# Reordering the head of a fused attention and FP4 feed-forward kernel: late pieces of x as jobs, zero rows by GpSimd, zeros multiplied in waits

## The chip, the cores and the metric

The kernel runs on one core of a Trainium2 chip. The metric is the device time of one execution in microseconds, the median of the runs shown. A core has a matrix engine (TensorE, PE in the profile), a vector engine (VectorE, DVE), a scalar engine that applies functions such as SiLU (ScalarE, ACT), a general engine (GpSimd, POOL) and a queue that mostly starts transfers (SyncE, SP). Each works through its own list of instructions in order, and they wait for one another by semaphores.

## The reference, cut to what matters

The input x has 2048 rows of 128 features.

```python
x_proj = silu(x @ W1 + b1)                      # (2048, 512)
u, v, q, k = split(x_proj, 4)                   # 16 heads of 8 features
scores = einsum('bqhd,bkhd->bhqk', qh, kh)      # 16 x 2048 x 2048
attn = silu(scores) / S
av = einsum('bhqk,bkhd->bqhd', attn, vh)
x = layernorm(x + (layernorm(av * u, gamma, beta) @ W2 + b2))
h = silu(fp4(x) @ fp4(w_gate).T) * (fp4(x) @ fp4(w_up).T)
out = layernorm(x + fp4(h) @ fp4(w_down).T)
```

SiLU is applied to every one of the 16 x 2048 x 2048 scores, 67 million values.

## The kernel before

**Layout.** x comes in five pieces (`X_LOADS`), is turned by TensorE against an identity matrix (L433) and copied from PSUM to `xT`. `k` and `q` are projected from `xT` in fp32, pass SiLU on ScalarE (`feat`) and are split by VectorE into three bf16 parts (`split`, L724 to L729). Transfers then lay these parts down in `k_stack` and `q_stack`, eight rows per head feature (`stack`, L255): six rows are products of parts, the last two must be zero. Such zero rows come from a memset for the first 256 columns (L864, L865, semaphore `stack_zeroed`) and from a transfer out of `zeros` for the others (`zero_rows`, L246). A unit is one such piece of k or q: (k, 0), (q, 0), (k, 256), (k, 768), (k, 1280), (k, 1792), and then the q pieces. The first three units are stacked half by SP and half by GpSimd (`SHARES`), the others by SP alone.

**The head.** `HEAD` (L226) is a list of operations (kind, start, width, PSUM bank) that TensorE goes through in order; after each one ScalarE takes the bank over (L649 to L660), a copy for `xT` and a SiLU for k, q and v. All five pieces of x, both first pieces of v and three pieces of k are in this list. Ahead of it stand six products of zeros (`WARM_UP`).

**The loop.** 256 steps (`STEPS`) go over chunks of queries, groups of heads and 16 tiles of keys. A step is `scores(at)`, two halves of 8 small products each into banks 0 to 5, taken by ScalarE with one SiLU of 128x1024 for a half (L682), then `times_v(at - 2)`, which multiplies the result of two steps ago by `v_pad`. Half n may be written only when SiLU n - 3 is done. Step i of the first chunk needs key tile i, so step 2 waits for the stack of (k, 256), step 6 for (k, 768), step 10 for (k, 1280) and step 14 for (k, 1792); `times_v(4)`, at step 6, needs the second v.

**Jobs.** `PREP_AT` says behind which step TensorE does a remaining piece of work: step: (kind, start). Before a job TensorE waits until the job before it has been taken out of its bank (`wait_job(k - 1)`, L518). ScalarE takes k, q, v and u jobs over after the first SiLU of the next step (L683, L684); VectorE takes the others.

**GpSimd and VectorE in the head.** GpSimd builds the identity, zeroes `v_pad` for the first four tiles (L314), prepares v's bias (L322 to L327), starts its share of the stack transfers, and copies v into `v_pad` (`pad_v`). VectorE zeroes small buffers, splits k and q, and zeroes the later quarters of `v_pad` between (`zero_v`).

## Time and profile before

| | |
|---|---|
| median of 3 runs | 520.77 us (518.68 to 522.34) |
| profiled execution | 521.81 us, of which the span from first to last instruction is 519.9 us |
| mean granted TensorE clock | 0.994 |
| PE busy | 500.2 us (96%) |
| ACT busy | 490.8 us (94%) |
| DVE busy | 210.8 us (41%) |
| POOL busy | 55.2 us (11%) |

Times in the rows are microseconds from the start of the span. Busy means that an instruction was running; an engine can be 96% busy and still be ahead of the one that sets the pace. A timeline row merges like instructions that follow each other: its second number is from the start of the first to the end of the last.

### The profile page before, as it was taken

To read this page: it belongs to the slowest core of one execution; us is meant where nothing else is said; L and a number is where in the kernel's file an instruction comes from. 1 tells how busy PE (TensorE), PEld (TensorE's weight loads), DVE (VectorE), ACT (ScalarE), POOL (GpSimd) and SP (SyncE) were. 2 spreads that over 40 slices of the span, in tenths; PEclk is the share of its full clock that TensorE was granted. 3 is DMA by queue.
4 is the path that set the end of the run, shared out by engine and by line. 5 is a ranking of instruction groups with operands and counts; after the bars stand their busy time and mean duration, and the time that the engine had idled before them with its cause. 6 is when DMAs were issued, how large, how long until landed. Compare 5 with 4: busy or idle time off the path is not lost.

```text
span 519.9 us, 19994 instructions
## 1 busy us (share of the span) xinstructions
PE 500.2 (96%) x9011; PEld 263.6 (51%) x9012; DVE 210.8 (41%) x621; ACT 490.8 (94%) x557; POOL 55.2 (11%) x148
## 2 busy tenths in 40 slices
PE   8899999999999999999999999999999999999995
PEld 4443344444444444444444444444367777777762
DVE  5446652343343332334333333334343434444445
ACT  4899999999999999999999999999999999999940
POOL 6600000101010100101010100101010101101010
PEclk9899999999999999999999999999999999999999
DMA  7831440000000000000000000000000000000000
GB/s 179 211 89 49 112 118 27 3 3 6 3 7 3 7 3 6 3 1 8 1 8 3 6 3 6 3 2 8 1 9 4 9 5 9 9 3 9 4 3 11
DMA packets 15155, 12.38 MB, mean 24 GB/s; under 512 B 1783, under 2 KB 14718, under 8 KB 15070
## 3 DMA queue, kind: packets, MB, share of 16 engines
q1 hardware_dynamic: 14088, 9.44, 7.2%
q0 software_dynamic: 688, 1.40, 1.1%
q8 instruction: 71, 1.16, 0.9%
q10 hardware_dynamic: 294, 0.26, 0.2%
q14 instruction: 14, 0.11, 0.1%
HBM read 1.92 MB, written 1.05 MB: 6 GB/s over the span
## 4 chain that ended last, share of the span: by engine, by line
ACT 54%; PE 31%; issue 11%; DVE 2%; DMA 1%; POOL 0%; SPq 0%; POOLq 0%; DVEq 0%
ACT attn L625 54%; PE ps L390 29%; PE ps L404 2%; DMA x_sb<-in_L_attn_x 1%; PE ps L433 0%; ACT v_sb L625 0%; POOL rstd_b L373 0%; DVE xn_b L751 0%; DVE stats_b L781 0%; ACT feat L625 0%; DVE xn_b L755 0%; DVE xn_b L757 0%; DVE xn_b L759 0%; SPq L275 0%; POOLq L126 0%
## 5 line engine op out<-in xcount | busy, mean ns | idle before, releaser
L625 ACT ACTIVATE attn<-ps 128x1024 f32<-128x1024 f32 x512 | 479.1, 1220 | 1.7 <-PE ps L390 1.5
L390 PE MATMUL ps<-attn,v_pad 128*32 128x256 f32 (+1 forms) x5120 | 275.2, 342 | 0.3 <-DVE wdown_t L925 0.2
L390 PE MATMUL ps<-q_stack,k_stack 64*128 64x256 bf16 (+1 forms) x2560 | 175.8, 251 | 11.8 <-ACT attn L625 2.6
L390 PEld LDWEIGHTS ps<-attn,v_pad 128*32 128x32 f32 x5120 | 132.4, 109 | 80.7 <-issue 39.4
L390 PEld LDWEIGHTS ps<-q_stack,k_stack 64*128 64x128 bf16 x2560 | 77.6, 94 | 138.1 <-ACT attn L625 93.5
L372 POOL TENSOR_TENSOR ve_a<-mv_a,eps_col 128x1 f32<-128x1 f32 x24 | 4.6, 190 | 244.5 <-DVE mv_a L783 244.5
L840 DVE TENSOR_TENSOR gate_a<-gate_a,ps 128x352 f32<-128x352 f32 x8 | 4.2, 521 | 53.1 <-PE ps L390 53.1
L372 POOL TENSOR_TENSOR ve_b<-mv_b,eps_col 128x1 f32<-128x1 f32 x24 | 4.6, 190 | 192.5 <-DVE mv_b L783 192.5
L840 DVE TENSOR_TENSOR gate_b<-gate_b,ps 128x352 f32<-128x352 f32 x7 | 3.7, 522 | 48.0 <-PE ps L390 48.0
L724 DVE CAST parts<-feat 128x512 bf16<-128x512 f32 (+1 forms) x10 | 3.9, 388 | 26.7 <-ACT feat L625 26.7
L390 PE MATMUL ps<-zeros 128*128 128x512 bf16 x47 | 12.2, 411 | 1.3 <-DVE zeros L862 1.2
L373 POOL TENSOR_TENSOR rstd_a<-ve_a,minus_half 128x1 f32<-128x1 f32 x24 | 13.3, 554 | 1.9
L373 POOL TENSOR_TENSOR rstd_b<-ve_b,minus_half 128x1 f32<-128x1 f32 x24 | 13.3, 553 | 1.9
L848 DVE COPY hqT_a<-ps 128x256 f32<-128x256 f32 x8 | 3.4, 424 | 22.4 <-PE ps L404 22.4
L390 PE MATMUL ps<-wgate_t,xqT 128*32 128x352 f32 (+1 forms) x122 | 12.5, 460 | 0.0
L390 PE MATMUL ps<-wup_t,xqT 128*32 128x352 f32 (+1 forms) x122 | 12.4, 459 | 0.0
L834 DVE COPY xqT<-ps 128x128 f32<-128x128 f32 x15 | 4.4, 292 | 16.9 <-PE ps L390 16.9
L848 DVE COPY hqT_b<-ps 128x256 f32<-128x256 f32 x7 | 3.0, 425 | 19.4 <-PE ps L404 19.4
L390 PE MATMUL ps<-xT,w_qk 128*32 128x512 f32 (+3 forms) x56 | 10.8, 582 | 0.0
L781 DVE BATCH_NORM_STATS2 stats_a<-ps 128x6 f32<-128x128 f32 x8 | 2.4, 299 | 19.4 <-PE ps L390 19.4
L625 ACT ACTIVATE feat<-ps,b_col 128x512 f32<-128x512 f32 (+1 forms) x10 | 7.5, 753 | 2.7 <-PE ps L390 2.7
L854 DVE TENSOR_TENSOR x1p_a<-ps,x_a 128x128 f32<-128x128 f32 x7 | 2.0, 292 | 19.6 <-PE ps L390 19.6
(156 smaller groups left out, 344.7 us busy)
## 6 DMA issues: line engine op xcount, KB each, us to landing
q_stack<-parts SPq DMA_DIRECT2D x18, 128.0 KB, 2.4
k_stack<-parts SPq DMA_DIRECT2D x15, 128.0 KB, 3.6
x_sb<-in_L_attn_x SPq DMA_DIRECT2D x3, 256.0 KB, 6.5
k_stack<-zeros SPq DMA_DIRECT2D x6, 128.0 KB, 5.5
q_stack<-zeros SPq DMA_DIRECT2D x6, 128.0 KB, 2.4
k_stack<-parts SPq DMA_DIRECT2D x9, 64.0 KB, 3.0
q_stack<-parts SPq DMA_DIRECT2D x9, 64.0 KB, 2.0
out<-x_a SPq DMA_DIRECT2D x8, 64.0 KB, 1.5
```

The source lines that it names most:

```text
L372: link(pool.tensor_tensor(r.ve[:, :], r.mv[:, which, 1:2], eps_col[:, :], ALU.add))
L373: pool.tensor_tensor(r.rstd[:, which:which + 1], r.ve[:, :], minus_half[:, :], ALU.pow).then_inc(rstd_ready, 1)
L390: return pe.matmul(to, lhsT, rhs, start=start, stop=stop, skip_group_check=True)
L404: return pe.transpose(ps[0:m, bank, a:a + n], src[:, 0:m], ident[0:n, 0:n])
L625: return act.activation(to, frm, ACT.Silu, **kw)
L724: dve.tensor_copy(p[:, 0, :], f).then_inc(split_done, 1)
L781: dve.bn_stats(r.stats[:, :], src)
L834: dve.tensor_copy(xqT[:, tile % 2, :], ps[:, bank, 0:P]).then_inc(job_by_vec, 1)
L840: dve.tensor_tensor(r.gate[:, :], r.gate[:, :], ps[:, bank, 0:FF], ALU.mult).then_inc(job_by_vec, 1)
L848: dve.tensor_copy(r.hqT[:, 0:2, :].rearrange("p t n -> p (t n)"), ps[:, bank, 0:2 * P])
L854: dve.tensor_tensor(r.x1p[:, :], ps[:, bank, 0:D], r.x1[:, :], ALU.add).then_inc(job_by_vec, 1)
```

## The change

1. `HEAD` loses the pieces (xT, 1280), (xT, 1792) and (v, 512); (k, 256) stands ahead of (xT, 768). The three become jobs at steps 1, 4 and 0. The other jobs up to (up, 0) stand one step later than before.
2. The last two pieces of x are loaded by SP behind the stacks of units 0 and 1 instead of ahead of them. They are turned by `turn_x` and copied by VectorE (`copy_xT`) instead of ScalarE.
3. The zero rows of unit 2, (k, 256), come from a GpSimd memset of columns 256 to 768 of `k_stack` (all eight rows, 8 x 512 bf16 for each partition) instead of two transfers by SP. GpSimd and SP wait for `k_zeroed`.
4. The first quarter of `v_pad` is zeroed half by GpSimd, two tiles, and half by VectorE, two tiles, behind the copy of `b1_col` (L873).
5. `FILL`: TensorE multiplies zeros once behind (xT, 0), three times behind (xT, 256), both into bank 7, and five times behind (k, 768) into bank 4.

The diff without the lines that only rename:

```diff
--- before.py
+++ after.py
@@ -92,9 +92,9 @@
 
-    PREP_AT = {2: ("k", 1280), 5: ("v", 2), 7: ("k", 1792), 9: ("v", 3), 11: ("u", 0), 13: ("q", 256),
-               15: ("u", 1), 17: ("q", 512), 19: ("u", 2), 21: ("q", 1024), 23: ("u", 3), 25: ("q", 1536),
-               27: ("w2", 0), 29: ("gate", 0), 31: ("up", 0), 33: ("down", 0)}
+    PREP_AT = {0: ("v", 1), 1: ("xT", 1280), 3: ("k", 1280), 4: ("xT", 1792), 6: ("v", 2), 8: ("k", 1792), 10: ("v", 3),
+               12: ("u", 0), 14: ("q", 256), 16: ("u", 1), 18: ("q", 512), 20: ("u", 2), 22: ("q", 1024),
+               24: ("u", 3), 26: ("q", 1536), 28: ("w2", 0), 30: ("gate", 0), 32: ("up", 0), 33: ("down", 0)}
 
     WIDE, DENSE = KT - 6, KT - 2
@@ -204,8 +204,8 @@
         split_done = sem("split_done")
-        stack_zeroed, v_zeroed_early, v_zeroed, v_padded = (sem("stack_zeroed"), sem("v_zeroed_early"), sem("v_zeroed"),
-                                                            sem("v_padded"))
+        stack_zeroed, k_zeroed, v_zeroed_early = sem("stack_zeroed"), sem("k_zeroed"), sem("v_zeroed_early")
+        v_zeroed, v_padded = sem("v_zeroed"), sem("v_padded")
         stacked = [sem(f"stacked{n}") for n in range(len(UNITS))]
         scores_ready, attn_ready = sem("scores_ready"), sem("attn_ready")
@@ -223,13 +223,14 @@
 
-        HEAD = [("xT", 0, 256, 0), ("k", 0, 256, 1), ("q", 0, 256, 2), ("xT", 256, 512, 3), ("xT", 768, 512, 4),
-                ("k", 256, 512, 5), ("xT", 1280, 512, 7), ("xT", 1792, 256, 0), ("v", 0, 512, 6),
-                ("k", 768, 512, 7), ("v", 512, 512, 6)]
+        HEAD = [("xT", 0, 256, 0), ("k", 0, 256, 1), ("q", 0, 256, 2), ("xT", 256, 512, 3), ("k", 256, 512, 5),
+                ("xT", 768, 512, 4), ("v", 0, 512, 6), ("k", 768, 512, 7)]
+
+        FILL = {("xT", 0): (1, 7), ("xT", 256): (3, 7), ("k", 768): (5, 4)}
         B1U_BANK = 2
         head_no = {job[:2]: n for n, job in enumerate(HEAD)}
-        X_LOADS = [(job[1], job[2]) for job in HEAD if job[0] == "xT"]
+        X_LOADS = [(0, 256), (256, 512), (768, 512), (1280, 512), (1792, 256)]
         xT_all = max(n for n, job in enumerate(HEAD) if job[0] == "xT") + 1
 
@@ -256,11 +257,10 @@
         SHARES = [((0, 1, 4), (2, 5, 3)), ((0, 2, 5), (1, 4, 3)), ((0, 1, 4), (2, 5, 3))]
-        BY_DMA = [len(SHARES[0][0]), len(SHARES[1][0]), len(SHARES[2][0]) + HD - TERMS]
 
             if n < len(SHARES):
-                eng.wait_ge(stacked[n], 16 * BY_DMA[n])
+                eng.wait_ge(stacked[n], 16 * len(SHARES[n][0]))
                 eng.wait_ge(stacked_by_pool[n], 16 * len(SHARES[n][1]))
                 eng.wait_ge(stacked[n], 16 * HD)
@@ -280,13 +280,14 @@
             load_x(sp, 2)
+            sp.wait_ge(stack_zeroed, 2)
+            for n in range(2):
+                stack(sp, n, SHARES[n][0])
+            load_x(sp, 3)
+            load_x(sp, 4)
+            sp.wait_ge(k_zeroed, 1)
+            stack(sp, 2, SHARES[2][0])
             sp.wait_ge(zeros_ready, 1)
-            for n in range(3, len(X_LOADS)):
-                load_x(sp, n)
-            zero_rows(sp, unit_no[("k", 256)])
-            sp.wait_ge(stack_zeroed, 2)
-            for n in range(3):
-                stack(sp, n, SHARES[n][0])
             for start in (768, 1280, 1792):
                 stack(sp, unit_no[("k", start)])
@@ -311,7 +312,8 @@
                                base=0, pattern=[[-1, P]], channel_multiplier=1).then_inc(ident_ready, 1)
-            pool.memset(v_pad[:, 0:TPC, :, :], 0.0).then_inc(v_zeroed_early, 1)
+            pool.memset(k_stack[:, :, 256:768], 0.0).then_inc(k_zeroed, 1)
+            pool.memset(v_pad[:, 0:2, :, :], 0.0).then_inc(v_zeroed_early, 1)
             pool.memset(ones_row[:, :], 1.0)
             pool.memset(minus_half[:, :], -0.5)
@@ -327,6 +329,7 @@
             pool.wait_ge(stack_zeroed, 2)
+            pool.wait_ge(k_zeroed, 1)
             for n in range(3):
 
@@ -335,7 +338,7 @@
                 else:
-                    pool.wait_ge(v_zeroed_early, 1)
+                    pool.wait_ge(v_zeroed_early, 2)
                 if ("v", c * CH) in head_no:
                 else:
@@ -418,9 +421,18 @@
 
+            def turn_x(bank, start, w):
+                pe.wait_ge(x_loaded[X_LOADS.index((start, w))], 16)
+                for i in range(w // P):
+                    last = pe.transpose(ps[:, bank, i * P:(i + 1) * P], x_sb[:, start // P + i, :], ident[:, :])
+                return last
+
+            def multiply_zeros(times, bank):
+                for _ in range(times):
+                    mm(ps[:, bank, :], zeros[:, 0:P], zeros[:, :])
+
             pe.wait_ge(zeros_ready, 1)
-            for _ in range(WARM_UP):
-                mm(ps[:, 7, :], zeros[:, 0:P], zeros[:, :])
+            multiply_zeros(WARM_UP, 7)
             pe.wait_ge(ident_ready, 1)
             for n, (kind, start, w, bank) in enumerate(HEAD):
@@ -428,9 +440,7 @@
                 if kind == "xT":
-                    pe.wait_ge(x_loaded[X_LOADS.index((start, w))], 16)
-                    for i in range(w // P):
-                        last = pe.transpose(ps[:, bank, i * P:(i + 1) * P], x_sb[:, start // P + i, :], ident[:, :])
+                    last = turn_x(bank, start, w)
                 else:
                                              if job[0] == "xT" and job[1] < start + w) + 1)
@@ -449,6 +459,7 @@
                     mm(ps[:, B1U_BANK, 0:1], b1_rows, ident[0:4, 0:1]).then_inc(b1_made, 1)
+                multiply_zeros(*FILL.get((kind, start), (0, 0)))
             pe.wait_ge(head_act, xT_all)
 
@@ -523,6 +534,8 @@
                     last = behind(kind, tile, bank)
+                elif kind == "xT":
+                    last = turn_x(bank, i, X_LOADS[[a for a, _ in X_LOADS].index(i)][1])
                 elif kind == "u":
                 elif kind in ("q", "k"):
@@ -589,8 +602,7 @@
             def keep_warm(piece):
-                for _ in range(KEEP_WARM.get(piece, 0)):
-                    mm(ps[:, 2, :], zeros[:, 0:P], zeros[:, :])
+                multiply_zeros(KEEP_WARM.get(piece, 0), 2)
 
             wait_job(job_no[("hqT", 0, TAIL - 1)])
@@ -871,6 +883,12 @@
             dve.tensor_copy(b1_col[:, 1:3], ps[:, 6, 1:3]).then_inc(b1_ready, 1)
+            dve.memset(v_pad[:, 2:TPC, :, :], 0.0).then_inc(v_zeroed_early, 1)
+
+            def copy_xT(start):
+                bank = wait_made("xT", start, None)
+                w = X_LOADS[[a for a, _ in X_LOADS].index(start)][1]
+                dve.tensor_copy(xT[:, start:start + w], ps[:, bank, 0:w]).then_inc(job_by_vec, 1)
 
                 dve.memset(v_pad[:, c * TPC:(c + 1) * TPC, :, :], 0.0).then_inc(v_zeroed, 1)
@@ -881,8 +899,10 @@
             split("k", 768)
+            copy_xT(1280)
             zero_v(1)
             split("k", 1280)
+            copy_xT(1792)
             zero_v(2)
```

## Rows read from the trace of the kernel before

**Rows 1.** The page, busy time, share and instructions of each engine

```profile
PE 500.2 (96%) x9011; PEld 263.6 (51%) x9012; DVE 210.8 (41%) x621; ACT 490.8 (94%) x557; POOL 55.2 (11%) x148
```

**Rows 2.** The page's costliest group: busy us, mean ns, then idle before it

```profile
L625 ACT ACTIVATE attn<-ps 128x1024 f32<-128x1024 f32 x512 | 479.1, 1220 | 1.7 <-PE ps L390 1.5
```

**Rows 3.** Waits of ACT from 30 to 500 us: total, times, longest

```profile
ACT attn L625 <- PE ps L390: 0.2, 1, 0.2
```

**Rows 4.** ACT's timeline: start, duration, instruction, idle before and its releaser

```profile
16.69 5.60 ACT L625 ACTIVATE attn<-ps 128x1024 f32<-128x1024 f32 x6
23.63 1.02 ACT L625 ACTIVATE attn<-ps 128x1024 f32<-128x1024 f32 x1 [1.34 <-PE ps L390]
24.55 0.68 ACT L625 ACTIVATE feat<-ps,b_col 128x512 f32<-128x512 f32 x1
...
29.97 1.02 ACT L625 ACTIVATE attn<-ps 128x1024 f32<-128x1024 f32 x1 [0.16 <-PE ps L390]
30.89 0.59 ACT L625 ACTIVATE v_sb<-ps 128x512 f32<-128x512 f32 x1
31.36 3.78 ACT L625 ACTIVATE attn<-ps 128x1024 f32<-128x1024 f32 x4
```

**Rows 5.** PE's timeline in the head, and one v job in the loop

```profile
1.19 2.74 PE L390 MATMUL ps<-zeros 128*128 128x512 bf16 x6 [1.19 <-DVE zeros L862]
...
5.00 2.07 PE L390 MATMUL ps<-xT,w_qk 128*128 128x256 f32 x4
6.87 1.06 PE L433 MATMUL ps<-ident,x_sb 128*128 128x128 f32 x4
8.63 1.12 PE L433 MATMUL ps<-ident,x_sb 128*128 128x128 f32 x4 [0.70 <-DMA x_sb<-in_L_attn_x]
9.54 1.92 PE L390 MATMUL ps<-xT,w_qk 128*128 128x512 f32 x2
...
11.90 1.09 PE L433 MATMUL ps<-ident,x_sb 128*128 128x128 f32 x6
12.82 1.06 PE L390 MATMUL ps<-w_sb,xT 128*128 128x128 f32 x8
...
13.94 1.02 PE L390 MATMUL ps<-xT,w_qk 128*128 128x512 f32 x2
...
16.09 0.83 PE L390 MATMUL ps<-q_stack,k_stack 64*128 64x256 bf16 x12
...
28.33 1.06 PE L390 MATMUL ps<-w_sb,xT 128*32 128x128 f32 x32
```

**Rows 6.** Two stretches, PE alone: length, busy (instructions), granted clock, DMA share, GB/s

```profile
16.09:20.13 4.04, 2.15 (x25) 0.89 0.99 240
20.13:23.20 3.07, 3.07 (x27) 0.59 1.08 234
```

**Rows 7.** PE's timeline in the tail, a run of products of zeros

```profile
502.20 4.70 PE L390 MATMUL ps<-zeros 128*128 128x512 bf16 x21 [0.16 <-issue]
```

**Rows 8.** SP's timeline, stack transfers of units 1 and 2

```profile
9.09 1.90 SPq L255 DMA_DIRECT2D q_stack<-parts  x3
12.66 2.45 SPq L255 DMA_DIRECT2D k_stack<-parts  x3
```

**Rows 9.** POOL's timeline, the memset that is cut and its first stack transfers

```profile
1.43 1.80 POOL L314 MEMSET v_pad<- 128x2048 f32 x1
...
7.70 1.77 POOL L255 DMA_DIRECT2D k_stack<-parts  x3 [0.88 <-DVE parts L724]
```

**Rows 10.** DVE's timeline, a memset of 1024 words and the first split

```profile
2.51 0.91 DVE L865 MEMSET q_stack<- 128x1024 uint32 x1 [0.16 <-issue]
...
6.76 0.29 DVE L724 CAST parts<-feat 128x256 bf16<-128x256 f32 x1 [1.53 <-ACT feat L625]
```

**Rows 11.** Q_stack's transfers issued from 10 to 12 us: time to landing

```profile
DMA to landing us min/median/max: 2.9/3.5/4.0
```

**Rows 12.** X_sb's transfers issued from 3.2 to 3.8 us: time to landing

```profile
DMA to landing us min/median/max: 7.3/7.3/7.4
```

## The prediction, made before the result was known

> **What bounds the kernel now.** I read the busy times first [rows 1]: PE 96% and ACT 94%, so either could set the pace. The group that costs most tells which: 512 SiLUs of scores take 479.1 us of ACT, and ACT stood idle ahead of them for 1.7 us in all [rows 2]. From 30 to 500 us its only wait for PE is 0.2 us [rows 3], and that is the one of 0.16 us at 29.97 [rows 4]. So from the first score SiLU, at 16.69, ACT is the clock of the whole kernel, one SiLU per 0.90 us or so (five more starts in a run of 5.60 us with a last one of about 1.02: 4.6 / 5 = 0.92). PE's 96% is slack spread thin. The reader should see three places where time can be had: the start at 16.69, the stalls of 1.34 and 0.16 us behind it (1.50 together) [rows 4], and other work on ACT between score SiLUs. The tail isn't touched. All else in the head counts only by what it does to these.
>
> What sets 16.69? PE's list of operations in the head [rows 5]. PE is busy almost without a break to the first scores at 16.09, and the first SiLU starts 0.60 us after them. The one visible gap is 0.70 us ahead of 8.63, where it waits for the third piece of x. Beside the order there is the clock: the same kind of product of 128x512 fp32 takes 1.92 us at 9.54 and 1.02 us at 13.94, and the four turns at 8.63 take 1.12 us where six take 1.09 us at 11.90. So PE ran at its lower level, 1.2 GHz, until about 11.5, and at 2.4 GHz behind it, though the granted clock of the first microseconds is shown as full. The trace has a second such stretch: over 16.09 to 20.13 PE was busy for only 2.15 of 4.04 us, and in 20.13 to 23.20 the granted clock is 0.59 [rows 6]. There lies the stall of 1.34 us: PE had times_v(0), the k job of step 2 and then the scores that ACT waited for, all at or near the lower level.
>
> **The change, part by part: the start.** I add up PE's list anew.
> - One product of zeros behind the first turn. A zero costs 2.74 / 6 = 0.46 us at the lower level [rows 5]; most lies in the wait for ACT's copy of xT, which k needs. Bounds 0 to 0.46, I take 0.2. The four turns of (xT, 256) then end at 7.93 + 0.20 = 8.13.
> - Three zeros, of which the wait for the copy (about 0.6 us) hides less than half at this level: 3 x 0.46 = 1.37, to 9.50. At the upper level a zero costs 4.70 / 21 = 0.22 us [rows 7] and the three fit the wait.
> - (k, 256) now runs here. Between 1.02 and 1.92 us; I take 1.02, since PE has by then been busy from 5.0 without the gap of 0.70, and before it rose some 2.9 us after that gap. To 10.52. The small b1 product behind it: 11.90 - 11.46 = 0.44, to 10.96.
> - (xT, 768), its load there since 8.6: 4 / 6 of 1.09 = 0.73, to 11.69. (v, 0): from 12.82 to 13.94, 1.12, to 12.81. (k, 768): 1.02, to 13.83; ACT's copy of (xT, 768), due by 12.4, doesn't hold it up. Gone are (xT, 1280), (xT, 1792) and (v, 512).
> - Five zeros at 0.22: 1.12, to 14.95. First SiLU 0.60 later: 15.55. That is 1.15 us earlier.
> The cover of this is the landing of the first two stacks. SP's transfers of q go out until 10.99 [rows 8], and those issued from 10 us landed 2.9 to 4.0 us later [rows 11], so at about 14.4: hidden behind 14.95, but a faster list than this gains at most 0.5 us more. With two loads of x and two zero transfers no longer ahead of them these landings should not get longer.
>
> **GpSimd and VectorE.** GpSimd's memset of 2048 words took 1.80 us [rows 9]. Now it does 8 x 512 bf16, as 2048 words another 1.80 us, or as 4096 elements 3.6 us, and then half of v_pad, 0.9 us. That puts its queue back by 0.9 us or by 2.7 us. Behind it stand v's bias, then the shares of the stacks of units 0, 1 and 2. Its first transfer was held back 0.88 us by the first split [rows 9], so a delay of 0.9 us costs nothing, one of 2.7 us puts the q share back by 1.8 us. The nearest row for the form is VectorE's zero memset of 8 x 256 bf16, shown as 1024 uint32 [rows 10]; I take the packed form.
>
> The Trainium skill (VectorE: DVE Perf Modes, section "Zero memsets can be issued as uint32 (trn2)") says that a memset takes one cycle an element whatever the type and describes the uint32 form for the Vector engine. Read strictly, GpSimd's would run over 4096 elements; that is one of the rivals below.
>
> VectorE's half of v_pad is 1024 words, 0.91 us by its row, in an idle time of 1.53 us ahead of the first split [rows 10]: nothing. If that cover were gone it would put back every stack by as much.
>
> **SP.** The two late loads of x stand between the stacks of unit 1 and unit 2, about 1.0 us of issuing from 10.99; unit 2's share then goes from 12.0 to some 13.8 instead of 12.66 to 15.11 [rows 8], and lands near 17, where step 2 wants it at about 19. The third and fourth piece of x were under way for up to 7.3 us [rows 12]; issued at 11.0 they land by 18.3 at the very worst, by 15 more likely. Both are hidden by what comes next.
>
> **The loop.** (v, 1) is now between score SiLUs: its row at 30.89 is followed by the next at 31.36, so 0.47 us of ACT, in full on the path. The copies of xT went to VectorE, which has time. The new thing is that two jobs stand in neighbouring steps. Job 1 (turn x 1280) waits for ScalarE to have taken job 0, and ScalarE does that only behind the first SiLU of step 1. Queued behind this wait on PE are the scores of step 2. By the sum: SiLU 2 from 17.35, v from 18.25 to 18.85, turns 0.73, scores 0.4 and on to ACT 0.2, so SiLU 4 at about 20.2, where ACT is free at 19.65: 0.55 us lost. The same pair stands at steps 3 and 4, with only two turns (0.36 us) and a k that ACT holds for 0.68 us [rows 4]: 0.2 us, and 0.15 for the k job itself. New stalls 0.9 us, bounds 0.3 to 1.8. In return PE has more to do right behind the head, v's 1.06 + 0.14 us (its row at 28.33) and the turns, so that the empty stretch that preceded the fall of the clock is half as long; I take the old 1.50 us as gone. Later jobs come one step later: (k, 1792) lands about 1.8 us later for step 14, which I count as still hidden, and the others have more room.
>
> Sum: -1.15 (start) - 1.50 (old stalls) + 0.90 (new ones) + 0.47 (v) = -1.28 us. The profiled execution took 521.81 us with a span of 519.9; this makes 520.5 with a span of 518.6. The median shown is 1.0 us lower than that execution, so 520.77 - 1.28 = 519.5.
>
> **The rivals.**
> - The clock rises early, and the fills cost nothing: zeros at 0.22, start held by the stacks at about 15.0 (-1.7), and only 0.4 us of new stalls. -1.7 - 1.5 + 0.4 + 0.47 = -2.3: 518.4. For it: PE's list has no gap left. Against it: it was busy from 1.19 to 7.93 already and stayed low.
> - Slower than before: the clock stays low. If (k, 256) takes 1.92 us, the first SiLU comes at 16.45 (-0.25), and if the fall of 20.13 to 23.20 comes again, the old 1.50 us stay and the new 0.90 are added. -0.25 + 0.90 + 0.47 = +1.1: 521.9. It decides as soon as the score stretch brings the lower level back. For it: zeros at the lower level are themselves work ahead of k. Against: the fall followed a stretch that is now fuller. The Trainium skill (TensorE: Matmul & The Clock Gate, section "What's actually happening") calls the throttled state the default that activity releases, which the turn from 1.92 to 1.02 us bears out; by it both this case and the one above are open.
> - GpSimd's memset by elements: q's share is last issued near 12.3 instead of 10.5 and lands at 15.3 to 16.3, so the first scores start at about 15.8, 0.85 later than in my sum: 519.5 + 0.85 = 520.4, the change without effect.
>
> **How the numbers follow.** The forecast has 0.4, the early rise 0.2, the low clock 0.2, the slow memset 0.2. The forecast is the likeliest's, 519.5. The range takes in the two outer cases, widened by the bounds of the new stalls on either side: 517.6 to 522.0. A measurement of this kernel can tell about 1% from no change, 5.2 us. All the time that this change could free, start and stalls together, is some 3.5 us, and no case costs over 2; outside 1% either way only an effect that I haven't seen would bring it: 0.03 each.
>
> **What would show each step.** First score SiLU at 15 to 16 instead of 16.69; the product for (k, 256) at about 9.5 with 1.0 us; a SiLU of v between the third and the fourth score SiLU; an idle time of ACT of about half a microsecond ahead of the fifth; the granted clock at 1.00 over the stretch that ends the first five steps; the GpSimd memset at 1.8 us. Wrong would make it a wait of the first scores for a stack, a wait of step 14 for (k, 1792), or a fall of the clock.

## The result and the profile after

The changed kernel's median is 522.89 us over 20 runs (521.78 to 526.43); that of before, over 20 runs beside it, is 520.55 us (518.68 to 522.66). The ratio is 1.0054 with a 95% interval of 1.004 to 1.0067: about 2.8 us slower by the ratio, 2.3 by the medians. Forecast was 519.5 us, 1.3 us faster, with a range of 517.6 to 522.0.

The profiled execution of the changed kernel took 521.78 us with a span of 519.8 us, and that of before 519.9. Compared alone these two would say that nothing happened. First ACT's timeline of the changed kernel (columns as in [rows 4], whose counterpart this is):

```profile
16.68 2.86 ACT L637 ACTIVATE attn<-ps 128x1024 f32<-128x1024 f32 x3 [0.72 <-PE ps L393]
19.40 0.62 ACT L637 ACTIVATE v_sb<-ps 128x512 f32<-128x512 f32 x1
...
21.09 3.77 ACT L637 ACTIVATE attn<-ps 128x1024 f32<-128x1024 f32 x4 [0.16 <-PE ps L393]
25.04 1.02 ACT L637 ACTIVATE attn<-ps 128x1024 f32<-128x1024 f32 x1 [0.17 <-PE ps L393]
...
31.68 1.02 ACT L637 ACTIVATE attn<-ps 128x1024 f32<-128x1024 f32 x1 [0.41 <-PE ps L393]
...
33.08 3.78 ACT L637 ACTIVATE attn<-ps 128x1024 f32<-128x1024 f32 x4
```

The start of the first score SiLU hasn't moved (16.68 against 16.69). The stall of 1.34 us is gone, small ones of 0.16, 0.17 and 0.41 stand in the loop now, and v (19.40) is between the third and the fourth score SiLU. PE's timeline, the counterpart of [rows 5]:

```profile
5.95 0.58 PE L393 MATMUL ps<-ident,magic_b 4*128 4x2 f32 x2 [1.37 <-DVE magic_b L880]
...
6.87 1.91 PE L393 MATMUL ps<-xT,w_qk 128*128 128x256 f32 x4
...
9.43 1.49 PE L393 MATMUL ps<-zeros 128*128 128x512 bf16 x3
10.71 1.65 PE L393 MATMUL ps<-xT,w_qk 128*128 128x512 f32 x2
...
15.07 1.24 PE L393 MATMUL ps<-zeros 128*128 128x512 bf16 x5
16.24 0.61 PE L393 MATMUL ps<-q_stack,k_stack 64*128 64x256 bf16 x8
...
20.07 0.66 PE L427 MATMUL ps<-ident,x_sb 128*128 128x128 f32 x4 [1.45 <-ACT v_sb L637]
```

k's first product starts at 6.87 instead of 5.00, and PE waits 1.37 us for a small copy by VectorE. In before the two small copies there were these:

```profile
3.78 0.27 DVE L868 COPY magic_b<-gate_b 4x128 f32<-4x128 f32 x1 [0.22 <-DMA gate_b<-in_L_attn_b]
3.98 0.26 DVE L871 COPY w_qk<-w_sb 128x128 f32<-128x128 f32 x1
```

VectorE and GpSimd of the changed kernel show what became of them (for the memsets see [rows 9 and 10]). VectorE:

```profile
1.43 0.91 DVE L876 MEMSET k_stack<- 128x1024 uint32 x1 [0.16 <-issue]
2.50 0.91 DVE L877 MEMSET q_stack<- 128x1024 uint32 x1 [0.16 <-issue]
...
3.77 2.12 DVE L880 COPY magic_b<-gate_b 4x128 f32<-4x128 f32 x1 [0.21 <-DMA gate_b<-in_L_attn_b]
3.96 2.00 DVE L883 COPY w_qk<-w_sb 128x128 f32<-128x128 f32 x1
```

GpSimd, of the same execution:

```profile
1.43 3.50 POOL L315 MEMSET k_stack<- 128x4096 bf16 x1
4.88 0.94 POOL L316 MEMSET v_pad<- 128x1024 f32 x1
...
9.57 1.77 POOL L256 DMA_DIRECT2D k_stack<-parts  x3 [0.82 <-DVE parts L736]
11.33 1.56 POOL L256 DMA_DIRECT2D q_stack<-parts  x3
```

The memset went over 4096 elements and took 3.50 us. The two copies of 0.27 and 0.26 us stand on VectorE as 2.12 and 2.00 us long, and both end within 0.15 us of the end of GpSimd's second memset (4.88 + 0.94 = 5.82). I call this the hold below; that GpSimd's memsets are its cause is tested by e12. VectorE's own memsets at 1.43 and 2.50 ran beside GpSimd's at their usual 0.91. And GpSimd's own stack transfers start at 9.57 instead of 7.70.

**Where in the span the time is.** One subtraction settles much. The row of four score SiLUs behind the third v (`x4`, at 33.08 above) is followed by 519.8 - 33.08 = 486.7 us to the end. In the experiments with the changed order of jobs below it is 518.9 - 32.23, 517.0 - 30.28, 515.8 - 29.11 and 522.6 - 35.91: 486.7 each time. In the order of before it is 519.9 - 31.36 = 488.5 [rows 4], and for another execution of before 517.2 - 28.64 = 488.6 (two SiLUs more, since v comes one step earlier). So all differences between the profiled executions, of different kernels and of one kernel, arise in the first 36 us.

### The profile page after: what moved, and what is told of

Read it like the earlier page. It is cut to its first block, busy times and chain, and to the rows that moved or that the text cites. A ratio compares the mean times of both kernels' runs of the same rounds, so it can differ in the third digit from the quotient of the medians.

```text
span 519.8 us, 20067 instructions
## 1 busy us (share of the span) xinstructions
PE 499.7 (96%) x9048; PEld 264.1 (51%) x9048; DVE 214.5 (41%) x624; ACT 490.1 (94%) x555; POOL 58.8 (11%) x149
## 3 DMA queue, kind: packets, MB, share of 16 engines
HBM read 1.92 MB, written 1.05 MB: 6 GB/s over the span
## 4 chain that ended last, share of the span: by engine, by line
ACT 52%; PE 32%; issue 10%; DVE 2%; DMA 1%; SPq 1%; POOL 0%; POOLq 0%; DVEq 0%
ACT attn L637 52%; PE ps L393 30%; PE ps L407 2%; SPq L256 1%; DMA k_stack<-parts 1%; PE ps L427 0%; DMA gate_b<-in_L_attn_b 0%; DVE magic_b L880 0%; ACT feat L637 0%; POOL rstd_b L376 0%; DVE xn_b L763 0%; DVE stats_b L793 0%; DVE xn_b L767 0%; DVE xn_b L771 0%; DVE xn_b L769 0%
## 5 line engine op out<-in xcount | busy, mean ns | idle before, releaser
L393 PE MATMUL ps<-zeros 128*128 128x512 bf16 x57 | 15.8, 423 | 1.2 <-DVE zeros L874 1.2
L393 PEld LDWEIGHTS ps<-zeros 128*128 128x128 bf16 x57 | 5.9, 106 | 8.2 <-issue 2.4
```

The lines of the kernel that those rows point to most:

```text
L393: return pe.matmul(to, lhsT, rhs, start=start, stop=stop, skip_group_check=True)
```

## The experiments

Each kernel was timed together with before. The medians of before in the four groups were 520.09 (e1 to e4), 520.18 (e5 to e8), 520.39 (e9 to e12) and 518.81 us (e13 to e15, 15 runs); 20 to 30 runs each in the first three. The last column counts the executions whose mean granted clock was under 0.996, which a fall to the lower level for some 3 us gives: of the profiles kept, those of before, e4, e12 and e14 have such a mean and show such a fall in the head, and no other shows one in its first 34 us.

The four groups ran on four chips, so a difference of medians across groups is less exact than one within a group. Before's own executions with a clock of 0.996 or more had medians of 519.2, 518.8, 518.7 and 518.5 us in the four groups, up to 0.7 us apart. I give the ratios to before beside such differences where they matter.

| kernel | median, us | ratio to before (95%) | first score SiLU, us | clock under 0.996 |
|---|---|---|---|---|
| changed | 522.89 | 1.0054 (1.004 to 1.0067) | 16.68 | 8 of 20 |
| e1_packed | 522.4 | 1.0045 (1.0027 to 1.0063) | 13.68 | 7 of 12 |
| e2_pool_only | 521.38 | 1.0011 (0.9994 to 1.0029) | 17.86 | 5 of 12 |
| e3_no_fill | 524.28 | 1.0089 (1.0066 to 1.0113) | 16.41 | 5 of 6 |
| e4_v_in_head | 522.86 | 1.006 (1.0037 to 1.0082) | 17.18 | 3 of 6 |
| e5_packed_x_early | 519.04 | 0.9989 (0.9975 to 1.0004) | 13.88 | 0 of 12 |
| e6_jobs_apart | 518.08 | 0.9974 (0.9962 to 0.9987) | 13.53 | 0 of 12 |
| e7_before_filled | 519.71 | 1.0002 (0.9989 to 1.0015) | 15.59 | 0 of 12 |
| e9_x_early_only | 520.88 | 1.002 (1.0002 to 1.0038) | 16.01 | 0 of 12 |
| e10_apart_no_fill | 519.53 | 0.9986 (0.9968 to 1.0003) | 15.06 | 0 of 12 |
| e11_apart_v_in_head | 519.51 | 0.9984 (0.9964 to 1.0004) | 16.45 | 5 of 12 |
| e12_copies_by_max | 524.42 | 1.0068 (1.0042 to 1.0095) | 16.48 | 7 of 7 |
| e13_gap_filled | 522.3 | 1.0057 (1.0037 to 1.0077) | 16.95 | 1 of 10 |

The start of the first score SiLU is that of the one profiled execution.

**e1_packed** (from the changed kernel):

```diff
-            pool.memset(k_stack[:, :, 256:768], 0.0).then_inc(k_zeroed, 1)
+            pool.memset(k_stack[:, :, 256:768].bitcast(U32), 0).then_inc(k_zeroed, 1)
```

> The changed kernel with GpSimd's memset of k_stack's columns 256 to 768 over the same bytes as 2048 uint32 instead of 4096 bf16. Theory (the memset holds VectorE's first two copies, which end at 5.9 instead of 4.2, and with them k and the whole head): the memset takes 1.8 us instead of 3.50, the copies end at about 4.2, k's first product starts at 5.3 instead of 6.87, the first score SiLU comes 1.4 to 1.6 us earlier than 16.68, and the median falls by as much, to about 521.4. Rival (the lost time is in the loop, by the added SiLU of v and the jobs in neighbouring steps): the start moves but ACT's stalls behind it grow by the same, and the median stays within 0.4 us of 522.9.

The mechanism was right and the forecast of the time wrong; the time came out nearer to the rival's. The memset took 1.80 us, VectorE's copies 0.34 and 0.25 us, k's product started at 4.85, and the first score SiLU came 3.0 us earlier, twice what was expected, since the clock was up earlier too (k's first product 1.13 us instead of 1.91).

```profile
1.43 1.80 POOL L315 MEMSET k_stack<- 128x2048 uint32 x1
...
4.04 0.25 DVE L883 COPY w_qk<-w_sb 128x128 f32<-128x128 f32 x1
```

Yet the span fell by 0.9 us and the median by 0.5, which the intervals of the two ratios do not tell apart. ACT's and PE's timelines show what took its place:

```profile
13.68 2.85 ACT L637 ACTIVATE attn<-ps 128x1024 f32<-128x1024 f32 x3 [1.72 <-PE ps L393]
...
19.57 3.77 ACT L637 ACTIVATE attn<-ps 128x1024 f32<-128x1024 f32 x4 [1.63 <-PE ps L393]
```

```profile
13.25 0.61 PE L393 MATMUL ps<-q_stack,k_stack 64*128 64x256 bf16 x8 [0.93 <-DMA q_stack<-parts]
...
19.14 0.61 PE L393 MATMUL ps<-q_stack,k_stack 64*128 64x256 bf16 x8 [1.40 <-DMA k_stack<-parts]
```

Step 2 waits for the stack of (k, 256). Its last five transfers, issued from 11.5 to 13.1 us, took this long to land:

```profile
DMA to landing us min/median/max: 5.0/5.8/6.0
```

SP had issued the late loads of x, its last two pieces, just ahead of them. And from 6 to 8 us, when in before these loads were under way, the transfers stood nearly still (columns: stretch, length, PE busy (count), clock, DMA share, GB/s):

```profile
6.00:7.00 1.00, 1.00 (x7) 1.00 0.02 6
7.00:8.00 1.00, 0.96 (x3) 1.00 0.03 6
```

**e2_pool_only**, from before: `pool.memset(k_stack[:, :, 256:768], 0.0)` ahead of the whole v_pad memset, the two zero transfers of unit 2 gone, with the waits that go with it.

> The kernel before with one part of the change: GpSimd's memset of 4096 bf16 in place of unit 2's two zero transfers, ahead of the whole v_pad memset. Theory (a GpSimd memset holds VectorE's copies): GpSimd zeroes without a break from 1.43 to about 6.7, VectorE's two copies that ended at 4.2 end at about 6.7, k's first product starts at 7.7 instead of 5.00, the first score SiLU comes 2.3 to 2.7 us later than 16.69 and the median rises by about as much, to 523. Rival (only GpSimd's own queue is late, its stack transfers by 3.5 us): VectorE's copies stay at 0.27 us, and scores wait for q's stack, at most 1 us later.

```profile
4.02 2.73 DVE L871 COPY magic_b<-gate_b 4x128 f32<-4x128 f32 x1 [0.46 <-DMA gate_b<-in_L_attn_b]
4.21 2.61 DVE L874 COPY w_qk<-w_sb 128x128 f32<-128x128 f32 x1
```

VectorE's copies ended within 0.15 us of the end of GpSimd's memsets (6.68); k's product started at 7.32. The hold is thus there in the old order too. The first score SiLU came 1.2 us later than in the rows of before, but 2.5 us later than in another execution of before (e8, below), which is the size expected. The median rose by 1.3 us, half of what I had expected, and the interval of the ratio takes in 1. The twelve executions fall into two sets, and the five with a clock under 0.996 are the faster ones here, 520.2 to 520.3 us against 521.3 to 522.0. So a low mean clock is no loss by itself. The profile is one of the others, and no trace shows what the five do differently.

**e3_no_fill**, from the changed kernel: `FILL = {}`.

> The changed kernel without the nine products of zeros in the head. Theory (the clock rises at the same place anyway, and the five zeros behind (k, 768) stand in front of the first scores): the first score SiLU comes about 1.2 us earlier, and the median falls by 0.8 to 1.2 us. Rival (the zeros hold the clock up through the first scores): the product of (k, 256) goes back to 1.9 us, a granted clock of 0.5 appears for about 3 us between 17 and 24 in most executions, and the median rises by 1 us or more.

The rival held, as far as it was seen. (k, 256) took 2.08 us, and though the first score SiLU came 0.27 us earlier, the median rose by 1.4 us. Five of six executions had a clock under 0.996. The profiled one had not, so the fall itself is here read from the executions' clocks, not from rows.

**e4_v_in_head**, from the changed kernel: `("v", 512, 512, 6)` at the end of `HEAD`, no job at step 0.

> The changed kernel with the second v back at the end of the head's list, behind the zeros, and no job at step 0. Theory (its place behind the start is worth what it costs): PE's list is 1.2 us longer, the first score SiLU comes 1.2 us later, ACT saves 0.47 us for v and some 0.5 us of the wait of job 1 for job 0: the median is within 0.5 us of the changed kernel's. Rival (the pair of jobs at steps 0 and 1 is the loss): the median falls by 1 us or more.

As in the theory: 522.86 against 522.89.

**e5_packed_x_early**, from e1_packed:

```diff
             load_x(sp, 2)
+            load_x(sp, 3)
+            load_x(sp, 4)
             sp.wait_ge(stack_zeroed, 2)
             for n in range(2):
                 stack(sp, n, SHARES[n][0])
-            load_x(sp, 3)
-            load_x(sp, 4)
```

> e1_packed with one more part undone: the last two loads of x again go out ahead of the stacks. Theory (in e1 the transfers stood nearly still from 6 to 8 us, and then the late loads went out just ahead of unit 2's stack, which took 5.9 us to land and held ACT's fifth SiLU back by 1.63 us): the landing of unit 2's stack falls to 3 to 4 us, ACT's wait ahead of the fifth score SiLU to 0.2 to 0.6 us, and the median is about 1 us below e1's 522.4. Rival (the loads cost the first stacks what they spare unit 2's): the first score SiLU goes from 13.7 to 14.5 or later, and the median stays.

It gave more than the theory said, 3.4 us by the medians (e1 and e5 ran in different groups), 2.9 by the ratios. The same five transfers of unit 2's stack landed within 3.3 to 4.6 us, against 5.0 to 6.0 in e1. SP also issued its three of them 1.2 us earlier, from 10.7 instead of 11.9, and no run parts the two. The wait of 1.63 us is one of 0.16; the first SiLU stays at 13.88; and no execution has a low clock any more. Its executions lie within 518.63 to 519.38 us, those of e1 within 520.0 to 524.45. The five of e1 with a clock of 0.996 or more have a median of 520.8, so some 1.7 us are there without a fall of the clock.

```profile
DMA to landing us min/median/max: 3.3/3.7/4.6
```

```profile
13.88 2.85 ACT L637 ACTIVATE attn<-ps 128x1024 f32<-128x1024 f32 x3 [1.79 <-PE ps L393]
...
18.30 3.77 ACT L637 ACTIVATE attn<-ps 128x1024 f32<-128x1024 f32 x4 [0.16 <-PE ps L393]
```

**e6_jobs_apart**, from e5:

```diff
-    PREP_AT = {0: ("v", 1), 1: ("xT", 1280), 3: ("k", 1280), 4: ("xT", 1792), 6: ...
+    PREP_AT = {0: ("v", 1), 2: ("xT", 1280), 3: ("k", 1280), 5: ("xT", 1792), 6: ...
```

> e5_packed_x_early with the jobs (xT, 1280) at step 2 and (xT, 1792) at step 5 instead of 1 and 4, so that none directly follows a job of ScalarE. Theory (PE stands for 1.4 us for job 0's SiLU and 0.5 us for that of the k job, which holds ACT back and lets the clock fall in a part of the executions): both gaps go, the sum of ACT's waits from the first score SiLU to 35 us falls by 0.5 to 0.9 us, fewer executions have a granted clock under 0.996, and the median falls by 1 to 1.5 us. Rival (the waits are those for stacks, the gap only shows them): no change over 0.3 us.

The waits behind the first SiLU are down to one of 0.16 us, the median falls by 1.0 us. The part about the clock could not be tested, for e5 had no low execution left. This is the version that beats both kernels: 518.08 us, 0.9974 of before. A part of that gain is that it has no falls: the 18 executions of before in this group with a clock of 0.996 or more have a median of 518.8, the 11 others one of 520.5.

```profile
16.73 5.67 ACT L637 ACTIVATE attn<-ps 128x1024 f32<-128x1024 f32 x6
22.30 0.68 ACT L637 ACTIVATE feat<-ps,b_col 128x512 f32<-128x512 f32 x1
...
27.71 1.02 ACT L637 ACTIVATE attn<-ps 128x1024 f32<-128x1024 f32 x1 [0.16 <-PE ps L393]
```

**e7_before_filled**, from before: zeros behind (xT, 256) and behind halves 2 to 5 of the scores.

> The kernel before with products of zeros alone added: one behind (xT, 256), which waits for the next load anyway, two each behind halves 2, 3 and 4 of the scores and one behind half 5, where PE waits for ACT, all into bank 7. Theory (the kernel before loses 1.3 to 2 us in those executions in which the clock falls between the first scores and step 3): no execution has the fall, the median comes to 519.0, against 520.1 to 520.5 for before, and the slowest to under 521. Rival (zeros in these waits come late for the stack or for times_v and cost more than they keep): the median is at or above 520.5.

Between the two. No execution had the fall, and the slowest was 520.86, as in the theory. But the median, 519.71, is above its 519.0 and the ratio 1.0002: the zeros cost what they kept. Beside the executions of before with a clock of 0.996 or more, median 518.8, e7 is 0.9 us slower. One such place is a new wait of 0.59 us of ACT ahead of its seventh score SiLU, whose scores started at 21.35, in e8 at 20.47.

**e8_before_again**, the kernel before, unchanged.

> The kernel before once more, for its profile. The times of its executions lie between 517.9 and 522.9 us, and the profiled one had a fall of the clock at 20 us. Theory (this spread is the clock in the first 25 us): an execution with a span near 517.3 has no stall of 1.34 us at 23.6, or has k's product of 1.0 us from the start and its first score SiLU before 16; the time from the start of the 17th score SiLU to the end is 485.8 us as in every other trace. Rival (the spread lies elsewhere): that last part differs by 1 us or more.

Its span is 517.2 us, 2.7 less than that of the execution in the rows of before. Here is where they go: the clock rose during the product of (k, 256) instead of behind it (1.30 us, in [rows 5] 1.92), the first score SiLU came at 15.38 instead of 16.69, and the stall of 1.34 us isn't there:

```profile
9.26 1.30 PE L390 MATMUL ps<-xT,w_qk 128*128 128x512 f32 x2
```

```profile
15.38 6.55 ACT L625 ACTIVATE attn<-ps 128x1024 f32<-128x1024 f32 x7
...
28.64 3.78 ACT L625 ACTIVATE attn<-ps 128x1024 f32<-128x1024 f32 x4
```

Of the 97 runs of before in these groups 43 had a clock under 0.996. The execution I predicted from, with 0.994, was of this kind.

**e9_x_early_only**, the changed kernel with the same edit of the loads as e5.

> The changed kernel with the last two loads of x ahead of the stacks again and GpSimd's memset left at 4096 elements. With e1 (short memset alone, 522.4) and e5 (both, 519.04) it fills the square. Theory (two causes that hide each other: a late head hides the late landing of unit 2's stack): the first score SiLU stays at 16.3 to 16.7, ACT's waits behind it stay near 0.75 us, and the median is 521.5 to 522.5, within 1.2 us of the changed kernel's 522.9. Rival (the late loads are the whole loss, the memset none): the median is 519.0 to 520 as in e5.

520.88: between theory and rival, nearer to the theory in its mechanism. The loads alone are worth 2.0 us (1.8 by the ratios), not 1.2 at most. The square of two memsets and two places of the loads is full:

| median, us | loads of x late | loads of x early |
|---|---|---|
| memset 3.50 us | 522.89 | 520.88 |
| memset 1.80 us | 522.4 | 519.04 |

By the ratios the short memset gives 0.5 us with the loads late and 1.6 with the loads early. The executions of e9 lie within 520.57 to 521.84 us, above all of e5's and, but for the one of 521.84, below all of the changed kernel's.

The first SiLU is at 16.01 here, with a list of PE that is done at 13.7. PE waits 1.87 us for the stack of q. That is the memset's second cost, GpSimd's own list:

```profile
15.58 0.61 PE L393 MATMUL ps<-q_stack,k_stack 64*128 64x256 bf16 x8 [1.87 <-DMA q_stack<-parts]
```

**e10_apart_no_fill**, e6 with `FILL = {}`.

> e6_jobs_apart without the nine products of zeros. Theory (the four early zeros bring the clock's rise forward, the five late ones only fill a wait for the stacks, so zeros pay in a head that isn't held back): k's first products and that of (k, 256) run longer, first score SiLU 14.5 to 15.5 instead of 13.53, a larger spread, and the median rises by 1 to 2 us from 518.08. Rival (the clock rises at the same time without them): the median stays within 0.3 us.

The theory held: (k, 256) took 2.07 us, first score SiLU at 15.06, the median 1.45 us higher. The spread did grow, but by one execution at each end. The intervals of the two ratios overlap, yet eleven of e10's twelve executions are above 519.0 us and eleven of e6's are under 518.9.

**e11_apart_v_in_head**, e6 with the second v at the end of `HEAD`.

> e6_jobs_apart with the second v at the end of the head's list instead of a job at step 0. Theory (PE waits about 1 us for the stacks at the head's end anyway, so v costs 1.2 us of PE of which some 0.4 to 1.0 are hidden, and ACT saves 0.47 us behind the start): within 0.5 us of 518.08. Rival (ACT's added SiLU is a real loss with nothing in return): the median falls to 517.6 or lower.

Neither: the median is 1.4 us higher (0.5 by the ratios, whose intervals overlap), and five of twelve executions had a low clock again. The executions fall into two sets, five from 517.78 to 518.82 us and seven from 519.47 on; the profiled one, with its first SiLU at 16.45, is the slowest of all. In e6 the v job lies in a stretch in which PE would otherwise wait between the first halves of the scores; that this is the reason was not tested.

**e12_copies_by_max**, from the changed kernel (the other copy likewise):

```diff
-            dve.tensor_copy(*w1_by_feature(1)).then_inc(w1_k_ready, 1)
+            w_out, w_in = w1_by_feature(1)
+            dve.tensor_tensor(w_out, w_in, w_in, ALU.max).then_inc(w1_k_ready, 1)
```

> The changed kernel with VectorE's two copies ahead of k (the one of b1_rows and the one of w1 for k) written as the larger of an operand and itself, two inputs from SBUF, same values; GpSimd's memset stays 3.50 us. Theory (a plain copy of VectorE can't run beside a GpSimd memset, another form can): the two take 0.2 to 0.4 us and end at 4.3 instead of 5.9, k's first product starts at 5.2 to 5.5 instead of 6.87, though GpSimd's list is as before. Rival (they wait for GpSimd's list or its data in some other way): they end at 5.9 as before.

The theory of the hold is shown by it: same place, same data, same GpSimd list, another form of instruction, and it runs at once:

```profile
3.63 0.38 DVE L881 TENSOR_TENSOR magic_b<-gate_b 4x128 f32<-4x128 f32 x1
3.94 0.37 DVE L885 TENSOR_TENSOR w_qk<-w_sb 128x128 f32<-128x128 f32 x1
```

One copy in this execution was left as a copy, but it reads PSUM and not SBUF. It ran in the middle of GpSimd's second memset (4.88 to 5.82) and wasn't held either:

```profile
5.02 0.16 DVE L887 COPY b_col<-ps 128x2 f32<-128x2 f32 x1 [0.71 <-PE ps L393]
```

k's product starts at 5.31. The time did not follow. PE's list ended at 13.1 and then stood for q's stack:

```profile
16.05 0.61 PE L393 MATMUL ps<-q_stack,k_stack 64*128 64x256 bf16 x8 [2.92 <-DMA q_stack<-parts]
```

GpSimd's share of it was issued from 10.79 on, for GpSimd's list is hardly earlier than before. In the profile the clock fell near 16.8, behind the idle 2.9 us, and stayed at 0.50 until past 20; the mean was low in all seven executions (0.987 to 0.995), and the median rose to 524.42. So a faster head in front of the same transfers gave nothing. That it made the kernel slower than the changed one, 524.42 against 522.89, the ratios (1.0068 and 1.0054, with overlapping intervals) do not show.

**e13_gap_filled**, from the changed kernel: five products of zeros into bank 6 ahead of job 1.

> The changed kernel with five more products of zeros, into the idle bank 6, in the 1.45 us for which PE waits ahead of job 1 for ScalarE to have taken job 0. Theory (in about half its executions the changed kernel's clock falls to the lower level behind this gap, which makes up most of the difference of 2.3 us in the median): no execution has a mean granted clock under 0.996, the spread shrinks from 4.6 to under 1.5 us, and the median is 521.8 to 522.2 against 522.89. Rival (the spread of the changed kernel has another cause, such as when transfers land): spread and median stay as they were.

The spread shrank from 4.6 to 1.3 us and one of ten executions had a low clock, against 8 of 20: in favour of the clock as the maker of the spread, but with ten executions no proof. The added zeros stand at 19.06, and in e14 (below) the clock had fallen before that, near 18.2, so they can't be what keeps such a fall away. The median, 522.3, is 0.6 us lower, and the ratio to the before beside it, 1.0057, isn't lower at all. The twelve executions of the changed kernel with a clock of 0.996 or more have a median of 522.1. So the change's loss is there without the falls.

**e14_after_look** and **e15_after_look2**, the changed kernel, unchanged.

> The changed kernel once more, for its profile: the first one was its fastest execution (span 519.8), others have spans up to 524.4 with mean granted clocks of 0.989 to 0.994. Theory: an execution with a span over 521 shows a granted clock of 0.5 for 3 us or more between 17 and 27 us and waits of ACT for the scores there, 1 to 4 us more than in the first profile, with the first score SiLU where it was (16.7, at most 1 us off). Rival: the first score SiLU itself comes later by what the span is longer.

> The same kernel as e14_after_look, for the case that one of the two is a fast execution again. The same theory and rival: what a span over 521 has more lies behind the first score SiLU at a granted clock of 0.5, or ahead of it.

e15 was like the first profile (span 520.0, first score SiLU 16.87). e14 was a long one, span 522.6, and both theory and rival have their share:

```profile
6.49 1.03 PE L393 MATMUL ps<-xT,w_qk 128*128 128x256 f32 x4
...
16.86 0.61 PE L393 MATMUL ps<-q_stack,k_stack 64*128 64x256 bf16 x8 [3.14 <-DMA q_stack<-parts]
```

```profile
17.29 1.94 ACT L637 ACTIVATE attn<-ps 128x1024 f32<-128x1024 f32 x2 [3.93 <-PE ps L393]
19.59 1.02 ACT L637 ACTIVATE attn<-ps 128x1024 f32<-128x1024 f32 x1 [0.36 <-PE ps L393]
...
22.85 1.94 ACT L637 ACTIVATE attn<-ps 128x1024 f32<-128x1024 f32 x2 [0.83 <-PE ps L393]
25.47 1.94 ACT L637 ACTIVATE attn<-ps 128x1024 f32<-128x1024 f32 x2 [0.68 <-PE ps L393]
27.87 1.02 ACT L637 ACTIVATE attn<-ps 128x1024 f32<-128x1024 f32 x1 [0.46 <-PE ps L393]
```

```profile
18.00:20.00 2.00, 1.98 (x32) 0.56 1.10 214
20.00:22.00 2.00, 0.85 (x4) 0.50 1.18 213
22.00:24.00 2.00, 2.00 (x18) 0.50 1.12 216
```

In this execution the clock rose early, PE's list was done at 13.7, and it waited 3.14 us for q's stack: the first SiLU comes 0.6 us later than in the first profile. Behind this idle time, from 18.2 to 25.0, the clock is at its lower level, and the waits of 0.36, 0.83, 0.68 and 0.46 us come with it. The idle time alone doesn't bring the fall: e13's profile waited 2.80 us at the same place and its clock stayed at 1.00. Set beside e9, which differs only in the loads of x and has its rows up to 13.7 at the same times, the part of the loads can be read off. GpSimd's last two transfers of q's stack, issued from 11.8 on, landed in

```profile
DMA to landing us min/median/max: 2.9/3.5/4.2
```

with the late loads beside them, and in 2.9 us at most in e9. The first scores start at 16.86 and 15.58; in e13, again with the late loads, at 16.52.

## Why the prediction was wrong

**The start (-1.15 forecast, 0.0 in the profile).** The first step that failed is the pricing of GpSimd's memset, "I take the packed form". It took 3.50 us, near the 3.6 of the other bound. That bound was a rival with 0.2, but priced wrongly: only as GpSimd's late share of q's stack (first scores at 15.8; e9 has 15.58 and e12 16.05, so this part was well sized, but for the late loads in e13 and e14, 16.52 and 16.86). What it left out is the hold on VectorE. I had looked at whether VectorE's memset of v_pad was covered, and not at whether VectorE could run beside the longer memset at all. In before the first of the two copies began right as GpSimd's last memset ended, so the rows of before don't show the hold. The Trainium skill (SBUF — State Buffer, section "Who interferes with whom") states it: VectorE's copies in its two-port modes and GpSimd exclude each other for a whole instruction, while an instruction with at most one input from SBUF outside these modes, such as a memset, and one with two inputs against a GpSimd that only writes don't. The traces agree with all three cases, by 2.12 us, 0.91 us and 0.38 us. They don't show which mode the copies ran in, and the hold lasted over two memsets, not one.

**SP ("these landings should not get longer").** This step failed too, and is the larger loss: undoing it gave 2.0 us with the long memset and 3.4 with the short one (1.8 and 2.9 by the ratios), where undoing the memset alone gave 0.5. I counted the late loads' issue time, 1.0 us, and that they land in time. I did not count what they do to the transfers they share the time with, unit 2's stack (5.0 to 6.0 us against 3.3 to 4.6) and GpSimd's share of q's (up to 4.2 against 2.9). The stretch they left, 6 to 8 us, then stood nearly empty.

**The old stall (-1.50).** Gone in the profile, as said, but it was no steady cost of before: e8 has no trace of it. With 43 of 97 runs of before at a low clock it could be counted at less than half. That the one profile at hand was of the slower kind was bad luck, but I took its stall as a cost of every execution. The changed kernel brought its own falls in 8 of 20.

**New stalls (+0.90) and v (+0.47).** 0.16 + 0.17 + 0.41 = 0.74 us. Apart, the jobs gave 1.0 us (e6). The mechanism was right and the sum near, the places not: ahead of the fifth SiLU 0.16 instead of 0.55, ahead of the fifteenth 0.41. v's place was worth nothing in the changed kernel (e4), and up to 1.4 us in e6 (e11).

**Zeros.** Right in sign: without them 1.4 us more, twice (e3, e10). (k, 256) took 1.65 us in the profile, between my bounds of 1.02 and 1.92; I had taken 1.02.

**The whole.** By medians, in the order e9, e5, e6: late loads 2.0, long memset 1.8, jobs side by side 1.0, together 4.8 us from the changed kernel to e6. By the ratios it is 1.8, 1.6 and 0.8, together 4.2. Without these three the change gains 1.4 us by the ratio of e6 and 2.1 by its medians; with them it is 2.3 to 2.8 us behind before. The loads and the memset hide each other, so their shares depend on which is undone first; only their sum doesn't. By the terms of the prediction the two profiles should differ by 0.0 - 1.50 + 0.74 + 0.47 = -0.3 us, and they differ by -0.1. So the sum holds for these two executions once the start is right. They stand for their kernels badly: the profile of before was one of its slower executions (521.81 us, median 520.55), that of the changed kernel its fastest (521.78, median 522.89). "A measurement of this kernel can tell about 1% from no change" was far too wide; the interval of the ratio is 0.27% from end to end. How much of e1's spread is the fall and how much the landing was not taken apart.

## What to carry to other kernels

Before a memset or a copy is moved to GpSimd, list what VectorE does in the same microseconds, by form of instruction; and write zero bytes in the widest type. Before a transfer is moved back because its data isn't needed yet, look at what will be under way when it goes out: a free stretch early is worth more than a full one later. Hold the new order against the executions of before without a fall as well, for a gain that only some executions have can be lost in the others. A head with several limits close together (here VectorE's copies, GpSimd's list, the landing of two stacks, the clock) shows the gain of an edit only when the others are undone too, so test in squares; and ask for the spread of the executions before taking a stall in one profile for a cost.

## What the runs showed of the hardware

- A VectorE copy from SBUF that came while the first of two GpSimd memsets ran (3.77, memset to 4.93) was let through only behind the second (5.82), not between them. In e2 it waited until 6.7 in the same way. VectorE's memsets (0.91 us), its form with two inputs (0.38) and its small copy out of PSUM (0.16, e12) ran beside GpSimd's memsets. GpSimd's next memset, of 1x128, took 0.33 us behind the held copies and 0.20 in e12, where no copy was held.
- GpSimd's memset costs by elements: 4096 bf16 3.50 us, the same bytes as 2048 uint32 1.80 us.
- The time at which TensorE's clock rises differs between executions of one kernel. In the changed kernel k's first product took 1.91 us in the first profile, where the clock rose only during the product of (k, 256) behind 10.71, and 1.03 us in e14, where it was up by 6.5. In before it rose near 11.5 in one execution and near 10 in the other (e8). The granted clock is shown as 1.00 in all of them for this time, so only the products' own durations tell.
- An early rise isn't a gain by itself: in e14 PE's list was done at 13.7 instead of 16.2, PE then waited 3.14 us for q's stack, and the clock fell 1.4 us behind that wait. In e13 it did not, behind 2.80 us.
